# Input preparation moved ahead of the small-tile products, and half of the rotary sum moved from GpSimd to VectorE, in a six-layer windowed-attention decoder

## The reference

```
for i in range(DEPTH):                      # 6 layers
    x = attn_layer(shift_tokens(x), Wqkv[i], q_scale[i], k_scale[i], Wo[i]) + x
    x = ffn_layer(shift_tokens(x), ...) + x
# attn_layer: 16 heads of 64, window of 32
q, k, v = split(x @ Wqkv)
q = l2norm(q) * qs;  k = l2norm(k) * ksc
q = q * cos * scale + rotate_half(q) * sin * scale
k = k * cos * inv   + rotate_half(k) * sin * inv
out = local_attention(q, k, v) @ Wo         # each window sees itself and the one before it
```

## Time and profile before

| what | us |
|---|---|
| median of 3 runs | 4236.15 |
| lowest and highest | 4233.85, 4240.07 |
| the profiled execution | 4238.05 |
| its span from first to last instruction | 4236.2 |

### The profile page before, as it was taken

How to read it: one execution, slowest core, us unless ns; L and a number is a source line. 1 busy time by engine, 2 the same in 40 slices (tenths; PEclk the granted TensorE clock), 3 DMA queues, 4 the chain that set the end, 5 groups by cost and what they waited for, 6 DMA issues and landing times.

```text
span 4236.2 us, 163553 instructions
## 1 busy us (share of the span) xinstructions
PE 3855.6 (91%) x61792; PEld 3145.5 (74%) x61792; DVE 3322.2 (78%) x8896; ACT 3215.2 (76%) x11601; POOL 3373.9 (80%) x2461
## 2 busy tenths in 40 slices
PE   7998886999989999889999899999899998999997
PEld 5665664877867777777777777777677777777786
DVE  7998887777777777777777687777777776877775
ACT  6988994888857888758888668887488886688884
POOL 4554447999968999869999689999599997899992
PEclk9999997999999999999999999999999999999999
DMA  3000001111112111111111121111111111111111
GB/s 83 0 0 1 0 0 31 35 37 35 36 37 52 36 36 35 38 52 35 36 35 35 35 55 35 36 36 37 51 37 35 37 35 36 39 35 35 37 35 43
DMA packets 302004, 145.50 MB, mean 34 GB/s; under 512 B 83989, under 2 KB 293779, under 8 KB 301459
## 3 DMA queue, kind: packets, MB, share of 16 engines
q1 hardware_dynamic: 301458, 137.25, 13.4%
HBM read 21.85 MB, written 2.10 MB: 6 GB/s over the span
## 4 chain that ended last, share of the span: by engine, by line
PE 56%; DVE 20%; ACT 11%; issue 10%; POOL 2%; DVEq 1%; SPq 0%; ACTq 0%; DMA 0%; POOLq 0%
PE bank L737 17%; PE bank L848 8%; PE pair L828 6%; PE pair L776 6%; PE bank L730 6%; ACT pair L1109 5%; PE pair L769 5%; PE pair L904 4%; DVE by_sin L1558 3%; PE bank L797 3%; DVE top L1506 3%; DVE top L1582 2%; DVE prob L1600 2%; DVE qk_parts L1481 2%; PE bank L920 1%
## 5 line engine op out<-in xcount | busy, mean ns | idle before, releaser
L1277 POOL TENSOR_TENSOR rnorm<-norm2g,neg_half 128x16 f32<-128x16 f32 x384 | 1115.5, 2905 | 147.1 <-DVE norm2g L1575 146.8
L1109 ACT ACTIVATE pair<-pair,top 128x64 f32<-128x64 f32 x3072 | 885.7, 290 | 265.0 <-DVE top L1582 265.0
L1269 POOL TENSOR_TENSOR rotated<-by_cos,by_sin 128x512 f32<-128x512 f32 x768 | 985.2, 1283 | 70.8 <-DVE by_sin L1558 68.8
L1289 POOL TENSOR_TENSOR rotated<-rotated,rnorm 128x512 f32<-128x512 f32 x768 | 784.9, 1043 | 0.5
L1100 ACT ACTIVATE squares<-bank 128x512 f32<-128x512 f32 x768 | 458.7, 597 | 355.9 <-DVE by_sin L1558 318.9
L737 PE MATMUL bank<-wqkv_high,xt_high 128*128 128x512 f32 (+1 forms) x1536 | 661.7, 431 | 12.7 <-ACT squares L1100 11.6
L1109 ACT ACTIVATION_READ_ACCUMULATOR pair<-pair,top 128x1 f32 x3072 | 638.7, 208 | 0.0
L776 PE MATMUL pair<-qk_t 64*32 64x64 f32 (+1 forms) x18432 | 608.9, 217 | 0.0
L1550 DVE TENSOR_TENSOR by_cos<-bank,rot_cos 128x512 f32<-128x512 f32 x768 | 528.2, 688 | 91.4 <-PE bank L737 64.4
L848 PE MATMUL bank<-wo_sb,prob_t 128*128 128x128 f32 x3072 | 531.4, 296 | 70.6 <-DVE y L1607 40.3
L828 PE MATMUL pair<-vout_all 64*64 64x64 f32 x6096 | 433.9, 227 | 118.3 <-DVE prob L1600 76.5
(11 more groups left out here) (151 smaller groups left out, 9004.1 us busy)
## 6 DMA issues: line engine op xcount, KB each, us to landing
vmoved<-vout_all SPq DMA_DIRECT2D x1152, 64.0 KB, 2.1
ctx_all<-vout_all SPq DMA_DIRECT2D x384, 64.0 KB, 2.1
wqkv_sb<-in_L_ffn_Wqkv_dram SPq DMA_DIRECT2D x36, 256.0 KB, 3.9
ctx_all<-y SPq DMA_DIRECT2D x48, 128.0 KB
ctx_all<-y SPq DMA_DIRECT2D x48, 127.0 KB
wo_sb<-in_L_ffn_Wo_dram SPq DMA_DIRECT2D x6, 512.0 KB, 10.2
out_dram<-y SPq DMA_DIRECT2D x8, 256.0 KB, 3.5
w_sb<-in_L_ffn_W_dram SPq DMA_DIRECT2D x6, 341.0 KB, 3.3
```

What stands on the lines that cost most here:

```text
L1109: last = nc.scalar.activation(at, at, ACT.Exp, bias=top[jl % 2][:, h:h + 1], accum_out=psum_raw[jl % 2][:, h:h + 1])
L1269: nc.gpsimd.tensor_tensor(rotated[j % 4][:, :, :, :], by_cos[j % 2][:, :, :, :], by_sin[j % 2][:, :, :, :], ALU.add).then_inc(c_rot, 1)
L1277: nc.gpsimd.tensor_tensor(rnorm[slot][:, :, :].rearrange("t g n -> t (g n)"), norm2g[slot][:, :, :].rearrange("t g n -> t (g n)"), neg_hal ...
L1289: nc.gpsimd.tensor_tensor(at, at, rnorm[slot][:, i, :].unsqueeze(2).to_broadcast([P, 2 * HG, DH]), ALU.mult).then_inc(c_unit, 1)
```

## The change

On TensorE `win_step` calls `win_turn_next` behind the output projection and ahead of scores and value sums. On ScalarE `win_copy_next` follows the copy of the heads and stands ahead of the exponentials. The sum into `rotated` is parted: GpSimd adds the keys' half (256 columns), VectorE the queries' half, as the last instruction of its step, and in the fill right behind the sine product. The semaphore of the sum becomes two, and GpSimd's multiplies wait for both. `win_cos` waits for the keys' half alone, the other half being on its own engine.

```
# TensorE
+            def win_whole_array(layer, it, j):
                 win_project(layer, it, j)
                 win_turn_probs(layer, it, j)
                 win_values(layer, it, j)
                 win_heads(layer, it, j)
                 win_project_out(layer, it, j)
+
+            def win_tiles(layer, it, j):
                 win_upper_scores(layer, it, j)
                 win_lower_scores(layer, it, j)
                 win_sum_values(layer, it, j)
+            def win_products(layer, it, j):
+                win_whole_array(layer, it, j)
+                win_tiles(layer, it, j)
             def win_step(layer, it, j):
-                win_products(layer, it, j)
+                win_whole_array(layer, it, j)
                 win_turn_next(layer, it, j)
+                win_tiles(layer, it, j)
# ScalarE
             def win_step(layer, it, j):
-                win_copies(layer, it, j)
+                win_copy_values(layer, it, j)
+                win_square(layer, it, j)
+                win_copy_heads(layer, it, j)
                 win_copy_next(layer, it, j)
+                win_exponentials(layer, it, j)
+                win_copy_sums(layer, it, j)
# GpSimd, win_rotate
-                    nc.gpsimd.tensor_tensor(rotated[j % 4][:, :, :, :], by_cos[j % 2][:, :, :, :], by_sin[j % 2][:, :, :, :], ALU.add).then_inc(c_rot, 1)
+                    nc.gpsimd.tensor_tensor(rotated[j % 4][:, 1, :, :], by_cos[j % 2][:, 1, :, :], by_sin[j % 2][:, 1, :, :], ALU.add).then_inc(c_rot, 1)
# GpSimd, win_unit
                     pool.wait_ge(c_rot, g + 2)
+                    pool.wait_ge(c_qrot, g + 2)
# VectorE
+            def win_rotate_queries(layer, it, j):
+                if here(it, j, 0):
+                    g = layer * GROUPS + it * STEPS + j
+                    dve.wait_ge(c_sin, g + 1)
+                    if has(it * STEPS + j - 4):
+
+                        dve.wait_ge(c_heads, g - 3)
+                    nc.vector.tensor_tensor(rotated[j % 4][:, 0, :, :], by_cos[j % 2][:, 0, :, :], by_sin[j % 2][:, 0, :, :], ALU.add).then_inc(c_qrot, 1)
# VectorE, win_step
                 win_add(layer, it, j)
+                win_rotate_queries(layer, it, j)
# VectorE, win_rotations (fill)
                 win_cos(layer, 0, j)
                 win_sin(layer, 0, j)
+                win_rotate_queries(layer, 0, j)
```

More of the change, by code:

```diff
@@ L372, in build @@
         c_rn = sem("c_rnorm")
-        c_rot = sem("c_rotated")
+        c_rot = sem("c_keys_rotated")
+        c_qrot = sem("c_queries_rotated")
         c_unit = sem("c_unit")
@@ L855, in xt_before @@
                 return min(NB, b + 4) if isinstance(b, int) else b + 4
-            def win_products(layer, it, j):
+            def win_whole_array(layer, it, j):
                 win_project(layer, it, j)
```

## The result

The changed kernel takes 4262.23 us (median of 4 runs, 4258.81 to 4266.61) beside 4236.5 us for the kernel before on the same chip: ratio 1.0061, 95% interval 1.0043 to 1.0078, so 26 us slower. The forecast was 4261. The sum is right; of its three terms the last sequences came out as forecast, the loop's was too large and the fill's had the wrong sign, as shown further down.

A forecast was written before the change was run, and what follows sets the result against it. Bound: TensorE, 56% of the chain, with VectorE's 1.01 us wait for ScalarE's input copy stalling it. Loop +20, last sequences +11 and fill -6 make +25 on the 4236.15 median: 4261 us, range 4208 to 4298.

The forecast's parts named there:

- the last sequences: Last two sequences of a layer, without an input: a blocked sum makes two steps about 7.8 us, not 7.30; +11 us.
- the loop's: Windowed loop: mean period of a four-step sequence 15.94 us against 15.82, over 174 periods; +20 us.
- the fill's: Fill of each layer: GpSimd's shorter sums on the chain save 1 us a layer net; -6 us in all.
- The input ahead of the tiles: Input's turn moved before scores: maxima 0.37 us later, but VectorE's 1.01 us wait for ScalarE's copy goes.
- Step 3: Last of a sequence's four steps, numbered 0 to 3; it prepares the input for two sequences ahead; 4.01 us before.
- rival (c): Input's turn costs 0.15 us more in its new place, delaying every maximum; +26, 4287 us; chance 0.12.
- the 4.1 named: Sign set for rival (c): step 3 taking over 4.1 us from product to product would make the prediction wrong.
- The stop: VectorE's sum of step 0 falls just inside GpSimd's first multiply and waits for its end; cos of step 1 9.88, not 9.14.
- rival (d): Odd steps' sums wait for all of rnorm, about 5100 us, or the sum for both multiplies, 4430; chance 0.04.
- (e): Rival: ScalarE's copy is released no earlier, the split stays late and the sum is added; 4360 us; chance 0.02.
- (a): Rival: in short periods the sum comes just ahead of the multiply and GpSimd waits instead; 4224 us; chance 0.2.
- (b): Rival: the sum is blocked in no period that counts and hides part of the loop's turn; 4204 us; chance 0.12.

## Why the prediction was right

**What bounded the kernel before: right.** The wait for ScalarE's copy was the costly one: ScalarE's order alone brings 131 us.

**The input ahead of the tiles: right to 0.1 us.** Step 3 to step 1 of the changed kernel, TensorE's timeline (it answers to the earlier trace rows):

```profile
2013.41 0.50 PE L738 MATMUL bank<-wqkv_high,xt_high 128*128 128x512 f32 x1
...
2017.76 0.50 PE L738 MATMUL bank<-wqkv_high,xt_high 128*128 128x512 f32 x1
...
2021.48 0.50 PE L738 MATMUL bank<-wqkv_high,xt_high 128*128 128x512 f32 x1
...
2025.70 0.50 PE L738 MATMUL bank<-wqkv_high,xt_high 128*128 128x512 f32 x1
...
2029.19 0.50 PE L738 MATMUL bank<-wqkv_high,xt_high 128*128 128x512 f32 x1
```

On the clock with 2013.41 at 0, forecast and measured:

| event | forecast | measured |
|---|---|---|
| maxima, step 3 | 3.81 | 3.78 |
| norm2g | 4.86 | 4.83 |
| split | 5.01 | 4.93 |
| cos, step 0 | 5.78 | 5.71 |
| probabilities | 7.18 | 7.11 |
| product, step 1 | 8.14 | 8.07 |
| the sum of step 0 | 8.77 | 8.89 |
| cos, step 1 | 9.88 | 9.89 |
| product, step 2 | 12.24 | 12.29 |
| next product, step 3 | 15.89 | 15.78 |

TensorE's input turn took the 0.37 us that it was given (2015.90 to 2016.27), against rival (c). (c)'s sign, though, showed: step 3 took 4.35 us from product to product, over the 4.1 named. The cause is another: TensorE's value sums of step 3 wait for probabilities that come late behind step 2's stop. With the input move alone step 3 takes 4.00 us (2022.09 to 2026.09 in its chain), and 4.01 with the sum in step 0 alone. The sign was badly chosen.

**The stop: right.** The sum of step 0 was named 3.91 after norm2g of step 3, just inside the first multiply. The multiply came 3.81 and the sum 4.06 after it. The sum took 1.07 us and cos of step 1 began 1.82 us after its product (2021.48 to 2023.30), against 1.7 forecast for a stop. Sums in odd steps are free of stops, against rival (d); the copy is released early, against (e); (a) and (b) needed sums of step 0 that aren't stopped. The Trainium skill (SBUF — State Buffer, section "SBUF: two separate sides") says that the shared port pair is locked for a whole instruction. The multiplies here agree with it; rnorm doesn't, since 2.90 us of it didn't hold up a sum that began 0.30 us after it. By the skill's sentence that sum would have taken about 2.6 us, an estimate from these two rows.

**The period: wrong by 0.1 us, which is most of the term.** The step that failed is TensorE's 3.65 us for step 2. I took it as what was left of the period before, and as TensorE's own work; it took 2029.19 - 2025.70 = 3.49, as some of the 3.65 was waiting that goes when the step starts late: from the turn of the heads to the scores it took 1.15 us before, 0.98 now. TensorE's timeline of step 2 before:

```profile
2046.24 0.60 PE L730 MATMUL bank<-cst,rotated 128*128 128x128 f32 x4
...
2047.39 0.24 PE L769 MATMUL pair<-band_b,ident_b 64*32 64x128 bf16 x4
```

And after:

```profile
2027.08 0.60 PE L731 MATMUL bank<-cst,rotated 128*128 128x128 f32 x4
...
2028.06 0.24 PE L770 MATMUL pair<-band_b,ident_b 64*32 64x128 bf16 x4
```

The plain period is 15.79 and not 15.89, the long one 15.88 and not 15.98. The mean is that of the kernel before within 0.01, where I had +0.12. That step 2's stop is caught up was right: the maxima of step 3 come at 3.78, and the kernel without a sum in step 2 has the same periods. The stop shows in step 3's 4.35, but step 1's product waits for VectorE's row and comes no later for it.

**The number of periods: the loop's first sequences were not looked at.** I gave all 174 periods the mean of the two steady ones. Before, the first four sequences of a layer don't pay for the loop's turn (13.8, 15.5, 15.6, 15.6). After, a sum is stopped from step 8 on (1.12 us), and that already falls into the first of these four. That is some +10 us, which happens to stand in for the +20 that the steady periods didn't give.

**The fill: wrong sign.** I had -6 us, with GpSimd's sum at 0.72 instead of 1.28 and an allowance for VectorE. GpSimd's timeline in the fourth layer's fill:

```profile
2483.22 0.97 POOL L1281 TENSOR_TENSOR rotated<-by_cos,by_sin 128x256 f32<-128x256 f32 x1 [0.38 <-DVE by_sin L1571]
```

VectorE's:

```profile
2483.18 0.42 DVE L1580 TENSOR_TENSOR rotated<-by_cos,by_sin 128x256 f32<-128x256 f32 x1
2483.52 1.22 DVE L1656 TENSOR_TENSOR y<-y,b_sb 128x512 f32<-128x512 f32 x1
```

Both halves start on the same release, the sine product, and so four of the five of each later fill meet: GpSimd's half takes 0.96 to 0.98, not 0.72. Once in each of these fills the feed-forward's bias, also of two operands in SBUF, then takes 1.22 where it took 0.68. The saving of the parted sum in the fill was 0.31 us and not 0.56, and VectorE lost more. Every kernel with the sum parted in all steps and two operands has 126.1 to 126.4 us in this stretch, every one without it 120.9 to 121.1; with one operand it is 124.9, so about 4 of the 5.5 us are VectorE's own time.

**The last steps: right** in size, +12.7 against +11.

**The sum: partly luck.** With +12, +13 and +5.5 in place of +20, +11 and -6 it is +30; the stretches for which I had no term take 7 off in the profiled run. That the total comes so near is luck in part, while the mechanism of the loop was seen as forecast. The range was badly drawn as well: its low end, 4208, lies above the 4204 of rival (b), from which it was to begin.

## What to carry to other kernels

Moving work off an engine that was busy 80% of the time but on 2% of the chain gained nothing in any kernel here. The receiving engine pays the instruction's length less the wait that follows it, and a stop on top where it falls beside one of the other engine's long adds or multiplies. Such costs don't simply add up: here the stop in step 0 hid what the other three sums cost. Try each place in the step for such an instruction: another one gave 109 us with the same work. When an order is changed on two engines at once, time each alone: here one half brought 131 us and the other cost 21, and there was a third place that cost nothing.

## What was not expected of the hardware

- Not every VectorE instruction is stopped at the same place: the add with two operands in SBUF was, while 768 reductions of the same size with one took 407 to 423 ns each beside all of GpSimd's work. It is no rule for one operand: the scaling of the earlier trace rows was stretched too.
- VectorE's stopped instruction ended 0.28 us behind the end of GpSimd's: all 366 sums over 0.5 us in the changed kernel, and 2029.54 against 2029.26 in the run with the sum behind the scaling; 0.15 for 128 columns. A sum that came as the first of two queued multiplies ended took 0.42 and the pair 2.30 (run of the sum alone): VectorE gets in between them.
- GpSimd pays too: a pair of multiplies with a VectorE sum waiting took 2.23 us instead of 2.04 to 2.05, and its own half of the sum up to 0.98 instead of 0.72.
